# Graph network block (GGNN, then attention) on 128 small graphs: the second half of the attention's gather gets another PSUM bank, and the probability transposes and gathers move in the hand-written order

## The chip, the cores and the metric

The kernel runs on one core of one Trainium2 chip. The metric is the device time of the whole launch in microseconds, lower is better; beside it stands the profile of one execution, with its span from the first to the last instruction. The matrix engine (TensorE) is PE in the rows, VectorE is DVE, ScalarE is ACT, GpSimd is POOL, SyncE is SP.

## The reference: what is computed

128 graphs of 128 nodes with 256 features each, and an adjacency per graph. Two layers, each a residual around a ReLU of a layer norm.

```python
h = relu(layernorm(x))                       # layer 0: gated graph network, 3 steps
for i in range(3):
    m = h @ weight[i]
    aggr = einsum('bst,bsd->btd', A, m)      # sum over neighbours
    h = gru(aggr, h, w_ih, w_hh, b_ih, b_hh)
x = x + h
h = relu(layernorm(x))                       # layer 1: graph attention
Wh = h @ W.T
e = leaky_relu((Wh @ a1)[:, :, None] + (Wh @ a2)[:, None, :])
x = x + softmax(where(adj, e, -inf)) @ Wh
```

## The kernel before

**Tiles.** Four graphs make a group (128 nodes on the partitions, or 512 = 4 x 128 node columns behind 128 features). Two groups, `a` = 0 and 1, make a pair `p`; there are 16 pairs. Every product is split in fp16 high and low parts and done as three matmuls (`products`, L318 in the profile).

**Slots and steps.** A pair has six slots of eight steps. Slots 0, 2, 4 are the three GRU layers of group 0, and slots 1, 3, 5 those of group 1. The eight steps of a slot are the gate products `hn0 r0 in0 z0 hn1 r1 in1 z1`, for feature half 0 and then 1, into the PSUM banks `hn_bank`, `r_bank`, `in_bank`, `z_bank`: six matmuls of 512 columns for `hn` and `in`, twelve for `r` and `z`. This is the bulk of PE's work.

**The side work.** Everything else (layer norms, neighbour sums, transposes, the attention of the pair before) is put behind the gate step by the table `SIDE`: the key is (slot, step), an entry is (stage, arguments, offset of the pair). Every engine walks the same table and issues its own part of each stage, strictly in that order, with waits on semaphores counted by pair. `LAST_SLOT_SIDE` takes the place of slot 5 in the last pair. In pair `p` the attention of pair `p - 1` runs (offset -1), so its stages occur in 15 of the walks; the attention of the last pair is in the list `TAIL` behind all slots.

**The attention stages that the change touches.** `softmax` (ACT) writes `prob`. `probs_transpose`: PE transposes `prob` into `s_bank` (L766, four transposes), ACT copies it to `pt_hi` (L858), DVE does three short operations (L964, L965, L967) and then writes `pt_lo` from `s_bank` and `pt_hi` (L970). `gather(p, a, half)`: PE waits for `pt_lo` and multiplies two graphs of the group (twelve matmuls of 128 columns, L318) into a bank, ACT copies that to `vt_hi` (L864), DVE writes `vt_lo` (L977). Both halves use `s_bank`, so the second half's matmuls wait until DVE has written the first half's `vt_lo`. `attend` multiplies `vt` with the attention's weight into `w_bank`. `residual(p, a, c)`: PE transposes the final state into `t_bank` (L749), DVE adds it to `x_res` (L921).

**The layer norm of the next pair.** At (4, 3) `stats_gnn` makes DVE take statistics of the next pair's input, from which POOL works out the factors in eleven small operations (L295 to L312). At (4, 5) `apply_gnn` makes ACT wait for them, write `relu_gnn` (L270, four operations) and its fp16 part `h_s` (L283, two). Behind that in the table stands `neighbours(1, 2, 1)`, whose ACT part is `nb_hi` (L347) and whose DVE part is `nb_lo` (L351). At (4, 6) `split_gnn` makes DVE write the low part of `h_s` (L263, two). The DVE operation of step `in` is `n_pre` (L887).

**The state.** `update` is three DVE operations (L896, L900, L903) behind ACT's `n_out` (L824) and `tanh_z` (L828); `split_state` splits the new state for the next layer.

The order of one slot is this loop, which all engines share:

```python
for step in range(len(STEPS)):
    gate(p, slot % 2, slot // 2, STEPS[step][:-1], step // 4)
    last_slot = slot == 2 * LAYERS - 1 and not exists(p + 1)
    for stage, *which, offset in (LAST_SLOT_SIDE if last_slot else SIDE).get((slot, step), ()):
        if stage in side and exists(p + offset):
            side[stage](p + offset, *which)
```

Of the kernel before, what the change touches and what calls it, by code (L numbers as in the profile page):

```python
# [75 lines left out]
    (2, 3): [("softmax", 0, -1)],  # L76
    (2, 4): [("update", 0, 1, 0, 0), ("split_state", 0, 2, 0, 0), ("transpose", 0, 2, 0, 0)],
    (2, 5): [("neighbours", 1, 1, 1, 0)],
    (2, 6): [("probs_transpose", 0, -1)],
    (3, 0): [("update", 0, 1, 1, 0), ("split_state", 0, 2, 1, 0), ("transpose", 0, 2, 1, 0)],  # L80
    (3, 1): [("gather", 0, 0, -1)],
    (3, 2): [("neighbours", 0, 2, 0, 0), ("dots", 1, 0, -1)],
# [6 lines left out]
    (4, 2): [("neighbours", 1, 2, 0, 0), ("softmax", 1, -1)],  # L89
    (4, 3): [("stats_gnn", 0, 1)],  # L90
    (4, 4): [("update", 0, 2, 0, 0)],
    (4, 5): [("probs_transpose", 1, -1), ("apply_gnn", 0, 1), ("neighbours", 1, 2, 1, 0)],
    (4, 6): [("split_gnn", 0, 1), ("first_transpose", 0, 0, 1), ("first_transpose", 0, 1, 1)],
    (4, 7): [("gather", 1, 0, -1)],
    (5, 0): [("residual", 0, 0, 0), ("update", 0, 2, 1, 0)],
    (5, 1): [("gather", 1, 1, -1)],
    (5, 2): [("attend", 1, 0, -1), ("neighbours", 0, 0, 0, 1), ("stats_gnn", 1, 1)],
    (5, 3): [("residual", 0, 1, 0), ("attend", 1, 1, -1), ("load_att", 1, 0), ("store", 1, -1)],
    (5, 4): [("update", 1, 2, 0, 0)],
    (5, 5): [("neighbours", 0, 0, 1, 1), ("stats_att", 0, 0)],  # L100
    (5, 6): [("apply_gnn", 1, 1)],
    (5, 7): [("split_gnn", 1, 1), ("first_transpose", 1, 0, 1), ("first_transpose", 1, 1, 1), ("apply_att", 0, 0)],
}

SETUP_SIDE = {
# [9 lines left out]
        ("first_transpose", 1, 1)]  # L115

LAST_SLOT_SIDE = {
    (5, 0): [("residual", 0, 0, 0), ("update", 0, 2, 1, 0)],
    (5, 1): [("gather", 1, 1, -1), ("attend", 1, 0, -1)],
    (5, 2): [("residual", 0, 1, 0), ("stats_att", 0, 0)],  # L120
    (5, 3): [("attend", 1, 1, -1), ("load_att", 1, 0), ("store", 1, -1)],
    (5, 4): [("update", 1, 2, 0, 0), ("apply_att", 0, 0)],
# [10 lines left out]
def per_group(p, a):  # L133
    return p * 2 + a + 1


def per_chunk(p, a, c):
    return p * 4 + 2 * a + c + 1
# [6 lines left out]
def per_gate(p, a, layer, c):  # L145
    return p * 12 + 4 * layer + 2 * a + c + 1
# [10 lines left out]
def wait_reached(engine, semaphore, count):  # L157

    if not (isinstance(count, int) and count < 1):
        engine.wait_ge(semaphore, count)  # L160


def graph_blocks(nc, x, adj, weight, w_ih, w_hh, b_ih, b_hh, att_w, att_a, out):
# [5 lines left out]
    with ctx:  # L169
# [3 lines left out]
        def sem(name):  # L173
            return ctx.enter_context(nc.semaphore(name))
# [35 lines left out]
        def bank(name):  # L210
            return ctx.enter_context(nc.psum_tensor(name, [P, 512], F32))

        nb_bank, t_bank = bank("nb_bank"), bank("t_bank")
# [11 lines left out]
        nb_hi_ready, nb_lo_ready, nb_done, x1_ready = sem("nb_hi_ready"), sem("nb_lo_ready"), sem("nb_done"), sem("x1_ready")  # L225
# [88 lines left out]
        def products(bank_ap, terms, start=True, stop=True):  # L314

            todo = [m for w_hi, w_lo, d_hi, d_lo in terms for m in ((w_hi, d_hi), (w_hi, d_lo), (w_lo, d_hi))]
            for i, (w, d) in enumerate(todo):
                last = nc.tensor.matmul(bank_ap, w, d, start=start and i == 0,  # L318
                                        stop=stop and i == len(todo) - 1)
            return last  # L320
# [298 lines left out]
        hn_bank, r_bank, in_bank, z_bank = bank("hn_bank"), bank("r_bank"), bank("in_bank"), bank("z_bank")  # L619
        w_bank, s_bank = bank("w_bank"), bank("s_bank")  # L620

        def after_gates(p):

            return isinstance(p, int) and p == pairs - 1
# [2 lines left out]
            return hn_bank if after_gates(p) and a == 1 else s_bank  # L627

        def gather_bank(p, half):
            return r_bank if after_gates(p) and half == 1 else s_bank  # L630

        def attend_bank(p, half):
            return (z_bank, nb_bank)[half] if after_gates(p) else w_bank
# [19 lines left out]
        u_lo_ready, vt_lo_ready, pt_lo_ready = sem("u_lo_ready"), sem("vt_lo_ready"), sem("pt_lo_ready")  # L653
# [28 lines left out]
        with nc.Block() as block:  # L682
# [28 lines left out]
            def _(pe):  # L711
# [33 lines left out]
                def residual(p, a, c):  # L745
                    pe.wait_ge(h_ready, per_gate(p, a, LAYERS - 1, c))
                    wait_reached(pe, x1_ready, per_chunk(p, a, c) - 1)
                    for b in range(GROUP):
                        last = nc.tensor.transpose(t_bank[:, b * P:(b + 1) * P], ht[a][:, c, b * P:(b + 1) * P], ident[:])  # L749
                    last.then_inc(res_t_done, 1)  # L750
# [18 lines left out]
                def gather(p, a, half):  # L769
                    n = per_chunk(p, a, half)  # L770
                    pe.wait_ge(u_lo_ready, per_group(p, a))
                    pe.wait_ge(pt_lo_ready, per_group(p, a))
                    if after_gates(p) and half == 1:
                        pe.wait_ge(tanh_r_ready, per_gate(p, 1, LAYERS - 1, 1))
                        if a == 1:
                            pe.wait_ge(vt_lo_ready, n - 2)
                    elif half == 1:
                        pe.wait_ge(vt_lo_ready, n - 1)
                    for k in range(KC):
                        for i in range(2):  # L780
                            b = 2 * half + i
                            target = gather_bank(p, half)[:, (2 * k + i) * P:(2 * k + i + 1) * P]
                            cols = slice(k * P, (k + 1) * P)
                            last = products(target, [(u_hi[a][:, b, cols], u_lo[a][:, b, cols],
                                                      pt_hi[:, b, :], pt_lo[:, b, :])])
                    last.then_inc(gather_done, 1)

                def attend(p, a, half):
# [13 lines left out]

                all_pairs(pe, gate, {
                    "residual": residual, "neighbours": lambda *which: neighbours_pe(pe, *which), "gather": gather,
                    "scores": scores, "probs_transpose": probs_transpose, "attend": attend})

            @block.scalar
            def _(act):
# [52 lines left out]
                def gather(p, a, half):  # L861
                    act.wait_ge(gather_done, per_chunk(p, a, half))
                    wait_reached(act, attend_done, per_chunk(p, a, 0) - 1)
                    nc.scalar.activation(vt_hi[:, :, 2 * P * half:2 * P * (half + 1)],  # L864
                                         gather_bank(p, half)[:].rearrange("p (k t) -> p k t", k=KC), ACT.Copy,
                                         scale=VSCALE / (HSCALE * PSCALE)).then_inc(vt_hi_ready, 1)
# [8 lines left out]
            def _(dve):  # L875
# [98 lines left out]
                def gather(p, a, half):  # L974
                    dve.wait_ge(vt_hi_ready, per_chunk(p, a, half))
                    part = slice(2 * P * half, 2 * P * (half + 1))
                    nc.vector.scalar_tensor_tensor(vt_lo[:, :, part],  # L977
                                                   gather_bank(p, half)[:].rearrange("p (k t) -> p k t", k=KC),
                                                   VSCALE / (HSCALE * PSCALE), vt_hi[:, :, part],
                                                   ALU.mult, ALU.subtract).then_inc(vt_lo_ready, 1)  # L980
# [57 lines left out]
```

## Time and profile before

| | |
|---|---|
| device time, median of 3 runs | 1867.82 us (1867.44 to 1868.47) |
| device time of the profiled execution | 1866.37 us |
| its span | 1864.6 us |
| PE busy | 1797.0 us, 96% of the span |
| DVE busy | 1420.2 us, 76% |
| ACT busy | 1028.3 us, 55% |
| POOL busy | 346.5 us, 19% |
| mean granted clock of PE | 0.993 |

Busy time of PE is that of pipelined matmuls: the row of a 512-column matmul shows 0.38 us, but the next one starts 0.216 us later. A wait of PE is therefore best read from start to start; the idle time that the profile prints is some 0.16 us less. One pair takes about 112.7 us.

### The profile page before, as it was taken

Reading aid. Unit: us, or ns where it says so; the run is one execution under the profiler, and the core shown is the slowest. Engines: PE = TensorE matmul, PEld = TensorE weight load, DVE = VectorE, ACT = ScalarE, POOL = GpSimd, SP = SyncE. Lnnn points to the kernel's source line nnn. Section 1 sums busy time; section 2 is a strip of 40 time slices with the busy share of each in tenths; the row PEclk is TensorE's granted clock in tenths of the full one; section 3 lists DMA queues with packets and bytes.
Section 4 is the critical chain, followed back from the end, with each engine's and each line's share of the span. In section 5 each row is a group of like instructions: output and inputs, shape, how many; then the busy total and the mean of one; then the engine's idle time right before and its main releaser. Section 6 shows DMA issues by size and latency. Waiting matters only on the chain.

```text
span 1864.6 us, 32405 instructions
## 1 busy us (share of the span) xinstructions
PE 1797.0 (96%) x10620; PEld 958.6 (51%) x10620; DVE 1420.2 (76%) x2801; ACT 1028.3 (55%) x1822; POOL 346.5 (19%) x778
## 2 busy tenths in 40 slices
PE   6999999999999999999999999999999999999995
PEld 5444555545555455555545555454554545555453
DVE  6667787777877877877777877777877777877776
ACT  5555555555555546555555556555555555555543
POOL 1022030311303122030310303113031220303101
PEclk9999999999999999999999999999999999999998
DMA  3323232322313223222222313223222322323111
GB/s 103 73 63 69 52 77 48 87 59 56 87 36 90 51 52 88 56 73 51 73 68 51 93 31 101 45 56 90 56 74 45 77 70 51 73 51 84 29 47 51
DMA packets 292000, 120.50 MB, mean 65 GB/s; under 512 B 207489, under 2 KB 291969, under 8 KB 291969
## 3 DMA queue, kind: packets, MB, share of 16 engines
q1 hardware_dynamic: 291968, 120.11, 26.7%
q8 instruction: 17, 0.28, 0.1%
q14 instruction: 15, 0.11, 0.0%
HBM read 52.96 MB, written 16.78 MB: 37 GB/s over the span
## 4 chain that ended last, share of the span: by engine, by line
issue 58%; POOL 13%; DVE 9%; PE 8%; ACT 7%; DMA 3%; POOLq 1%; ACTq 0%; DVEq 0%; SPq 0%
DMA ht_s<-h_s 3%; PE z_bank L318 3%; PE r_bank L318 2%; POOL ln_gnn L310 2%; DVE n_pre L887 2%; POOL ln_att L310 2%; ACT relu_gnn L270 2%; DVE dot_terms L933 1%; PE hn_bank L318 1%; ACT tanh_r L819 1%; PE in_bank L318 1%; ACT relu_att L270 1%; DVE stats_att L248 1%; ACT u_hi L845 1%; POOL ln_att L306 1%
## 5 line engine op out<-in xcount | busy, mean ns | idle before, releaser
L824 ACT ACTIVATE n_out<-n_pre,bih 128x512 f32<-128x512 f32 x192 | 137.9, 718 | 255.0 <-DVE n_pre L887 252.8
L318 PE MATMUL hn_bank<-ht_s,wh_hi 128*128 128x512 f16 x768 | 228.4, 379 | 1.7 <-PEq L426 1.7
L318 PE MATMUL r_bank<-ht_s,wh_hi 128*128 128x512 f16 x768 | 228.4, 379 | 0.0
L318 PE MATMUL z_bank<-ht_s,wh_hi 128*128 128x512 f16 x768 | 228.4, 379 | 0.0
L882 DVE SCALAR_TENSOR_TENSOR n_pre<-tanh_r,hn_b 128x512 f32<-128x512 f32 x192 | 146.2, 761 | 68.1 <-ACT tanh_r L819 65.1
L814 ACT ACTIVATE hn_b<-hn_bank,b_hn,down 128x512 f32<-128x512 f32 x192 | 147.5, 768 | 77.8 <-PE hn_bank L318 77.8
L819 ACT ACTIVATE tanh_r<-r_bank,b_rz,down 128x512 f32<-128x512 f32 x192 | 147.4, 768 | 68.9 <-PE r_bank L318 68.8
L833 ACT ACTIVATE ht_s<-ht 128x512 f16<-128x512 f32 x128 | 80.5, 629 | 186.7 <-DVE ht L903 186.7
L351 DVE TENSOR_TENSOR nb_lo<-nb_bank,nb_hi 128x512 f16<-128x512 f32 x192 | 131.2, 683 | 67.7 <-ACT nb_hi L347 67.6
L295 POOL TENSOR_TENSOR ln_gnn<-stats_gnn 128x4 f32<-128x4 f32 x32 | 12.9, 404 | 901.9 <-DVE stats_gnn L248 901.9
L828 ACT ACTIVATE tanh_z<-z_bank,b_rz,down 128x512 f32<-128x512 f32 x192 | 146.9, 765 | 35.9 <-PE z_bank L318 35.9
L909 DVE SCALAR_TENSOR_TENSOR ht_s<-ht,ht_s 128x512 f16<-128x512 f32 x128 | 88.6, 692 | 97.1 <-ACT ht_s L833 97.1
L347 ACT ACTIVATE nb_hi<-nb_bank 128x512 f16<-128x512 f32 x192 | 113.0, 589 | 82.9 <-PE nb_bank L333 82.9
L896 DVE SCALAR_TENSOR_TENSOR diff<-ht,n_out 128x512 f32<-128x512 f32 x192 | 131.9, 687 | 30.1 <-ACT n_out L824 29.8
L900 DVE SCALAR_TENSOR_TENSOR diff<-tanh_z,diff 128x512 f32<-128x512 f32 x192 | 133.7, 696 | 15.8 <-ACT tanh_z L828 9.2
L318 PE MATMUL r_bank<-ht_s,wh_lo 128*128 128x512 f16 x384 | 145.5, 379 | 0.0
L318 PE MATMUL r_bank<-nb_hi,wi_hi 128*128 128x512 f16 x384 | 145.5, 379 | 0.0
L318 PE MATMUL r_bank<-nb_lo,wi_hi 128*128 128x512 f16 x384 | 145.5, 379 | 0.0
L318 PE MATMUL r_bank<-nb_hi,wi_lo 128*128 128x512 f16 x384 | 145.5, 379 | 0.0
L318 PE MATMUL in_bank<-nb_hi,wi_hi 128*128 128x512 f16 x384 | 145.5, 379 | 0.0
L318 PE MATMUL in_bank<-nb_lo,wi_hi 128*128 128x512 f16 x384 | 145.5, 379 | 0.0
L318 PE MATMUL in_bank<-nb_hi,wi_lo 128*128 128x512 f16 x384 | 145.5, 379 | 0.0
(180 smaller groups left out, 4053.2 us busy)
## 6 DMA issues: line engine op xcount, KB each, us to landing
x_in<-in_x_dram SPq DMA_DIRECT2D x32, 512.0 KB, 4.1
x_res<-in_x_dram SPq DMA_DIRECT2D x32, 512.0 KB, 4.1
out_dram<-x_out SPq DMA_DIRECT2D x32, 512.0 KB, 5.0
adj_in<-in_adj_dram SPq DMA_DIRECT2D x32, 256.0 KB, 4.2
adj_att<-in_adj_dram SPq DMA_DIRECT2D x32, 256.0 KB, 4.3
h_s<-ht_s SPq DMA_TRANSPOSE x128, 3.0
ht_s<-h_s SPq DMA_TRANSPOSE x64, 3.2
raw_ih<-in_L_gnn_w_ih_dram SPq DMA_DIRECT2D x2, 384.0 KB, 3.9
```

Source lines behind the costliest of these rows:

```text
L318: last = nc.tensor.matmul(bank_ap, w, d, start=start and i == 0, stop=stop and i == len(todo) - 1)
L347: nc.scalar.activation(nb_hi[a][:, c, :], nb_bank[:], ACT.Copy).then_inc(nb_hi_ready, 1)
L351: nc.vector.tensor_tensor(nb_lo[a][:, c, :], nb_bank[:], nb_hi[a][:, c, :], ALU.subtract).then_inc(nb_lo_ready, 1)
L814: nc.scalar.activation(hn_b[c][:], hn_bank[:], ACT.Identity, bias=b_hn[:, c:c + 1], scale=down_gate).then_inc(hn_ready, 1)
L819: nc.scalar.activation(tanh_r[c][:], r_bank[:], ACT.Tanh, bias=b_rz[:, c:c + 1], scale=down_half).then_inc(tanh_r_ready, 1)
L824: nc.scalar.activation(n_out[c][:], n_pre[c][:], ACT.Tanh, bias=bih[:, 4 + c:5 + c]).then_inc(n_ready, 1)
L828: nc.scalar.activation(tanh_z[c][:], z_bank[:], ACT.Tanh, bias=b_rz[:, 2 + c:3 + c], scale=down_half).then_inc(tanh_z_ready, 1)
L833: nc.scalar.activation(ht_s[layer % 2][a][:, c, 0, :], ht[a][:, c, :], ACT.Copy, scale=HSCALE).then_inc(ht_hi_ready, 1)
L882: nc.vector.scalar_tensor_tensor(n_pre[c][:], tanh_r[c][:], 1.0, hn_b[c][:], ALU.add, ALU.mult).then_inc(rn_ready, 1)
L896: nc.vector.scalar_tensor_tensor(diff[c][:], ht[a][:, c, :], 1.0 / HSCALE if layer == 0 else 1.0, n_out[c][:], ALU.mult, ALU.subtract).the ...
L900: nc.vector.scalar_tensor_tensor(diff[c][:], tanh_z[c][:], 1.0, diff[c][:], ALU.add, ALU.mult).then_inc(zdiff_ready, 1)
L909: nc.vector.scalar_tensor_tensor(ht_s[q][a][:, c, 1, :], ht[a][:, c, :], HSCALE, ht_s[q][a][:, c, 0, :], ALU.mult, ALU.subtract).then_inc( ...
```

## The change

Three edits go together. `gather_bank` gives the second half `t_bank`, the bank of the residual's transposes, in all pairs but the last (where it had `r_bank` already). The waits follow: the second half waits for what last read `t_bank` (the residual of group 1 for group 0, the second half of group 0 for group 1), and `residual` of group 0, half 0 waits for the `vt_lo` that reads `t_bank`. The table moves four things: `probs_transpose(0)` from (2, 6) to (2, 7); `probs_transpose(1)` from (4, 5), where it stood ahead of `apply_gnn`, to (4, 6), behind `split_gnn`; `gather(1, 0)` from (4, 7) and `gather(1, 1)` from (5, 1), both to (5, 0); `residual(0, 0)` from (5, 0) to (5, 1).

```diff
-    (2, 6): [("probs_transpose", 0, -1)],
-    (4, 5): [("probs_transpose", 1, -1), ("apply_gnn", 0, 1), ("neighbours", 1, 2, 1, 0)],
-    (4, 7): [("gather", 1, 0, -1)],
+    (4, 6): [("split_gnn", 0, 1), ("first_transpose", 0, 0, 1), ("first_transpose", 0, 1, 1), ("probs_transpose", 1, -1)],
+    (5, 0): [("gather", 1, 0, -1), ("gather", 1, 1, -1), ("update", 0, 2, 1, 0)],
...
         def gather_bank(p, half):
-            return r_bank if after_gates(p) and half == 1 else s_bank
+            if half == 0:
+                return s_bank
+            return r_bank if after_gates(p) else t_bank
...
                     wait_reached(pe, x1_ready, per_chunk(p, a, c) - 1)
+                    if a == 0 and c == 0:
+                        wait_reached(pe, vt_lo_ready, per_chunk(p - 1, 1, 1))
...
+                    elif half == 1 and a == 0:
+                        pe.wait_ge(x1_ready, per_chunk(p, 1, 1))
                     elif half == 1:
-                        pe.wait_ge(vt_lo_ready, n - 1)
+                        pe.wait_ge(vt_lo_ready, n - 2)
```

On ACT, from slot 4, step `r1`, to slot 5, before (line numbers are those of each kernel; the rows REGISTER_ALU and ISA are waits and counters):

```order
L819 ACTIVATE tanh_r<-r_bank,b_rz,down 128x512
L858 ACTIVATE pt_hi<-s_bank 128x512
L160 ISA
L278 ISA
L270 ACTIVATE relu_gnn<-x_in,ln_gnn 128x256 x4
L283 ACTIVATE h_s<-relu_gnn 128x512 x2
L346 REGISTER_ALU
L347 ACTIVATE nb_hi<-nb_bank 128x512
L824 ACTIVATE n_out<-n_pre,bih 128x512
L828 ACTIVATE tanh_z<-z_bank,b_rz,down 128x512
L862 REGISTER_ALU
L864 ACTIVATE vt_hi<-s_bank 128x2x256
```

and after:

```order
L824 ACTIVATE tanh_r<-r_bank,b_rz,down 128x512
L159 ISA
L277 ISA
L269 ACTIVATE relu_gnn<-x_in,ln_gnn 128x256 x4
L282 ACTIVATE h_s<-relu_gnn 128x512 x2
L345 REGISTER_ALU
L346 ACTIVATE nb_hi<-nb_bank 128x512
L863 ACTIVATE pt_hi<-s_bank 128x512
L829 ACTIVATE n_out<-n_pre,bih 128x512
L833 ACTIVATE tanh_z<-z_bank,b_rz,down 128x512
L819 ACTIVATE hn_b<-hn_bank,b_hn,down 128x512
L867 REGISTER_ALU
```

The copy `pt_hi` stood ahead of the next pair's layer norm; it now stands behind the layer norm's six operations and `nb_hi`.

On DVE, the same place, before:

```order
L882 SCALAR_TENSOR_TENSOR n_pre<-tanh_r,hn_b 128x512
L964 TENSOR_SCALAR row_live<-row_max,down 128x4
L965 RECIPROCAL row_inv<-row_sum 128x4
L967 TENSOR_TENSOR row_scale<-row_live,row_inv 128x4
L970 SCALAR_TENSOR_TENSOR pt_lo<-s_bank,pt_hi 128x512
L350 REGISTER_ALU
L351 TENSOR_TENSOR nb_lo<-nb_bank,nb_hi 128x512
L887 SCALAR_TENSOR_TENSOR n_pre<-in_bank,down,n_pre 128x512
L261 REGISTER_ALU
L263 SCALAR_TENSOR_TENSOR h_s<-relu_gnn,h_s 128x512 x2
L977 SCALAR_TENSOR_TENSOR vt_lo<-s_bank,vt_hi 128x2x256
```

and after:

```order
L887 SCALAR_TENSOR_TENSOR n_pre<-tanh_r,hn_b 128x512
L349 REGISTER_ALU
L350 TENSOR_TENSOR nb_lo<-nb_bank,nb_hi 128x512
L892 SCALAR_TENSOR_TENSOR n_pre<-in_bank,down,n_pre 128x512
L260 REGISTER_ALU
L262 SCALAR_TENSOR_TENSOR h_s<-relu_gnn,h_s 128x512 x2
L969 TENSOR_SCALAR row_live<-row_max,down 128x4
L970 RECIPROCAL row_inv<-row_sum 128x4
L972 TENSOR_TENSOR row_scale<-row_live,row_inv 128x4
L975 SCALAR_TENSOR_TENSOR pt_lo<-s_bank,pt_hi 128x512
L982 SCALAR_TENSOR_TENSOR vt_lo<-s_bank,vt_hi 128x2x256
L982 SCALAR_TENSOR_TENSOR vt_lo<-t_bank,vt_hi 128x2x256
```

`pt_lo` with its three short operations went behind `nb_lo`, `n_pre` and both `h_s`, and the two `vt_lo` now follow each other.

On ACT at the end of slot 2, before:

```order
L347 ACTIVATE nb_hi<-nb_bank 128x512
L858 ACTIVATE pt_hi<-s_bank 128x512
L824 ACTIVATE n_out<-n_pre,bih 128x512
L828 ACTIVATE tanh_z<-z_bank,b_rz,down 128x512
L814 ACTIVATE hn_b<-hn_bank,b_hn,down 128x512
```

and after:

```order
L346 ACTIVATE nb_hi<-nb_bank 128x512
L829 ACTIVATE n_out<-n_pre,bih 128x512
L833 ACTIVATE tanh_z<-z_bank,b_rz,down 128x512
L863 ACTIVATE pt_hi<-s_bank 128x512
L819 ACTIVATE hn_b<-hn_bank,b_hn,down 128x512
```

`pt_hi` went behind `n_out` and `tanh_z`. DVE's order there is unchanged: `pt_lo` stands right ahead of the three operations of `update`.

## Rows read from the trace of the kernel before

**Rows 1.** The page: busy time of each engine, share of the span, instructions

```profile
PE 1797.0 (96%) x10620; PEld 958.6 (51%) x10620; DVE 1420.2 (76%) x2801; ACT 1028.3 (55%) x1822; POOL 346.5 (19%) x778
```

**Rows 2.** Waits of PE, whole span: us in total, times, longest us

```profile
PE s_bank L318 <- DVE vt_lo L977: 22.8, 14, 1.8
PE s_bank L766 <- ACT prob L851: 12.1, 16, 5.5
PE setup_bank L484 <- DVE peaks L528: 6.6, 1, 6.6
...
PE t_bank L749 <- DVE x_res L921: 3.1, 1, 3.1
```

**Rows 3.** Timeline of PE, pair 9, slots 4 to 5: start us, us, engine, line

```profile
1131.65 0.22 PE L318 MATMUL s_bank<-pt_hi,u_hi 128*128 128x128 f16 x1
...
1132.32 0.59 PE L318 MATMUL hn_bank<-ht_s,wh_hi 128*128 128x512 f16 x2
...
1133.61 0.60 PE L749 MATMUL t_bank<-ident,ht 128*128 128x128 f32 x4
1134.05 0.59 PE L318 MATMUL r_bank<-ht_s,wh_hi 128*128 128x512 f16 x2
...
1138.37 0.22 PE L318 MATMUL s_bank<-pt_hi,u_hi 128*128 128x128 f16 x1 [1.57 <-DVE vt_lo L977]
...
1139.04 0.38 PE L318 MATMUL in_bank<-nb_hi,wi_hi 128*128 128x512 f16 x1
```

**Rows 4.** Timeline of POOL, pair 9, slot 4: the layer norm's last factor

```profile
1130.18 0.20 POOL L312 TENSOR_TENSOR ln_gnn<-ln_gnn 128x4 f32<-128x4 f32 x1
```

**Rows 5.** Timeline of ACT, same stretch

```profile
1130.41 2.08 ACT L270 ACTIVATE relu_gnn<-x_in,ln_gnn 128x256 f32<-128x256 f32 x4 [2.07 <-POOL ln_gnn L312]
...
1133.63 0.58 ACT L347 ACTIVATE nb_hi<-nb_bank 128x512 f16<-128x512 f32 x1
...
1136.92 0.58 ACT L864 ACTIVATE vt_hi<-s_bank 128x512 f16<-128x512 f32 x1
```

**Rows 6.** Timeline of DVE, same stretch

```profile
1128.60 0.22 DVE L964 TENSOR_SCALAR row_live<-row_max,down 128x4 f32<-128x4 f32 x1
...
1129.01 0.68 DVE L970 SCALAR_TENSOR_TENSOR pt_lo<-s_bank,pt_hi 128x512 f16<-128x512 f32 x1
1134.24 0.69 DVE L351 TENSOR_TENSOR nb_lo<-nb_bank,nb_hi 128x512 f16<-128x512 f32 x1 [4.55 <-ACT nb_hi L347]
...
1135.51 1.28 DVE L263 SCALAR_TENSOR_TENSOR h_s<-relu_gnn,h_s 128x512 f16<-128x512 f32 x2
1137.53 0.69 DVE L977 SCALAR_TENSOR_TENSOR vt_lo<-s_bank,vt_hi 128x512 f16<-128x512 f32 x1 [0.74 <-ACT vt_hi L864]
```

**Rows 7.** Timeline of PE, pair 2, slots 2 to 3

```profile
301.65 0.66 PE L766 MATMUL s_bank<-ident,prob 128*128 128x128 f32 x4 [0.45 <-ACT prob L851]
302.14 0.59 PE L318 MATMUL z_bank<-ht_s,wh_hi 128*128 128x512 f16 x2
...
308.61 0.22 PE L318 MATMUL s_bank<-pt_hi,u_hi 128*128 128x128 f16 x1
```

**Rows 8.** Timeline of ACT, same stretch

```profile
303.81 0.59 ACT L858 ACTIVATE pt_hi<-s_bank 128x512 f16<-128x512 f32 x1
...
306.14 0.76 ACT L828 ACTIVATE tanh_z<-z_bank,b_rz,down 128x512 f32<-128x512 f32 x1
```

**Rows 9.** Timeline of DVE, same stretch

```profile
305.81 0.68 DVE L970 SCALAR_TENSOR_TENSOR pt_lo<-s_bank,pt_hi 128x512 f16<-128x512 f32 x1
306.41 0.68 DVE L896 SCALAR_TENSOR_TENSOR diff<-ht,n_out 128x512 f32<-128x512 f32 x1
```

**Rows 10.** Stretches at a low clock: length, busy times, then PEclk

```profile
17.01:20.25 3.24, 3.24 (x10) 2.76 (x11) 3.07 (x11) 0.00 (x0) 1.67 (x10) 0.50 0.00 0
1831.95:1849.70 17.75, 5.82 (x34) 4.41 (x35) 15.02 (x52) 5.64 (x15) 4.12 (x11) 0.52 0.00 0
```

**Rows 11.** Operations of one POOL line: ns min/median/max

```profile
L306 POOL TENSOR_TENSOR ln_gnn<-ln_gnn x32: 198/200/522, 19.6 to 1711.4; 128x4 f32<-128x4 f32 x32
```

More of the change, by code:

```diff
@@ L91 @@
     (4, 4): [("update", 0, 2, 0, 0)],
-    (4, 5): [("probs_transpose", 1, -1), ("apply_gnn", 0, 1), ("neighbours", 1, 2, 1, 0)],
-    (4, 6): [("split_gnn", 0, 1), ("first_transpose", 0, 0, 1), ("first_transpose", 0, 1, 1)],
-    (4, 7): [("gather", 1, 0, -1)],
-    (5, 0): [("residual", 0, 0, 0), ("update", 0, 2, 1, 0)],
-    (5, 1): [("gather", 1, 1, -1)],
+    (4, 5): [("apply_gnn", 0, 1), ("neighbours", 1, 2, 1, 0)],
+    (4, 6): [("split_gnn", 0, 1), ("first_transpose", 0, 0, 1), ("first_transpose", 0, 1, 1), ("probs_transpose", 1, -1)],
+    (5, 0): [("gather", 1, 0, -1), ("gather", 1, 1, -1), ("update", 0, 2, 1, 0)],
+    (5, 1): [("residual", 0, 0, 0)],
     (5, 2): [("attend", 1, 0, -1), ("neighbours", 0, 0, 0, 1), ("stats_gnn", 1, 1)],
@@ L102 @@
     (5, 7): [("split_gnn", 1, 1), ("first_transpose", 1, 0, 1), ("first_transpose", 1, 1, 1), ("apply_att", 0, 0)],
+    (2, 7): [("probs_transpose", 0, -1)],
 }
@@ L117 @@
 LAST_SLOT_SIDE = {
-    (5, 0): [("residual", 0, 0, 0), ("update", 0, 2, 1, 0)],
-    (5, 1): [("gather", 1, 1, -1), ("attend", 1, 0, -1)],
+    (5, 0): [("gather", 1, 0, -1), ("gather", 1, 1, -1), ("update", 0, 2, 1, 0)],
+    (5, 1): [("residual", 0, 0, 0), ("attend", 1, 0, -1)],
     (5, 2): [("residual", 0, 1, 0), ("stats_att", 0, 0)],
```

## The prediction, made before the changed kernel ran

> **What bounds the kernel now.** I read the page's busy times first: PE is busy 96% of the span [rows 1], so the time is PE's own work plus the places where it stands still, and an edit pays or costs only what it does to those. The waits of PE come next [rows 2]. Two recur: 22.8 us in 14 waits where the second gather waits for `vt_lo`, and 12.1 us in 16 where the probability transposes wait for `prob`; one of these is the tail's 5.5 us, so the other 15 are 0.44 us each. From start to start both kinds are about 0.16 us longer: 0.60 us for the second. The setup's and the tail's waits are single ones and the change does not reach them.
>
> Then the timeline at the first wait, in a pair that stands for the others. PE issues the first gather of group 1 at 1131.65, `hn` at 1132.32, the residual's transposes at 1133.61, `r` at 1134.05. Twelve matmuls at the 0.215 us that six of `hn` show ((1133.61 - 1132.32)/6) end that at 1136.63, but the second gather starts at 1138.37: 1.74 us lost [rows 3]. The bank is the reason only in form. `vt_lo` is written at 1137.53, right behind a `vt_hi` of 1136.92 [rows 5, 6], though PE had finished that gather at 1132.3. Between them ACT was behind: it waited 2.07 us for POOL's last layer-norm factor (1130.18 to 1130.38) [rows 4], ran the layer norm, and got to `nb_hi` at 1133.63 [rows 5]; DVE sat idle 4.55 us for that `nb_hi` [rows 6]. What is late in this stretch is the chain POOL, layer norm, `nb_hi`, `nb_lo`, `n_pre`, `h_s`, and everything behind it in the order of ACT and DVE. The probability copy is not behind it now: `pt_lo` was written at 1129.01 to 1129.70 [rows 6].
>
> **The change at slots 4 to 5.** It puts the probability copy behind that chain. ACT runs `pt_hi` after `nb_hi` (ends 1134.21); 0.59 us for such a copy [rows 8], so it is there by 1134.8 and delays nobody, since ACT's next operation waits for DVE anyway. DVE is the later one: it ends the two `h_s` at 1135.51 + 1.28 = 1136.79, then the three short operations take 0.41 us (1128.60 to 1129.01) and `pt_lo` 0.68 us [rows 6]. So `pt_lo` is written at 1137.88. PE starts a gather 0.15 us after the DVE operation that releases it (1138.37 against 1138.22) [rows 3, 6], less about 0.08 us by which DVE operations overlap: 1137.95.
>
> PE meets this wait sooner. The 0.67 us of the first gather are gone from ahead of `hn`, which starts at 1131.65 and ends at 1132.94. Behind it stands the first gather now, and PE waits from 1132.94 to 1137.95: **5.0 us where it waited 1.74**. The second gather follows at once, since `t_bank` is free: that part of the change works. What PE did before its old wait, it now does after: gather 0.67, gather 0.67, `r` 2.58, transposes 0.44, and `in` starts at 1142.31 instead of 1139.04 [rows 3]. That is **3.27 us later per pair**. Nothing takes it back: what waits behind the gather on PE is all of slot 5, and a PE that is busy 96% has no slack to give. The residual's new wait is covered: both `vt_lo` follow ACT's two copies of 0.58 us and end near 1140.8, 1 us before the transposes are due at 1141.9.
>
> The old wait has 14 instances for 15 pairs, because the last pair normalises no next input; there the copy is not late and I cost the edit at nothing. 14 x 3.27 = **+45.8 us**.
>
> **The change at slots 2 to 3.** PE's 0.60 us wait for `prob` goes, as `z` covers it (twelve matmuls, 2.6 us). What is late next is `pt_lo`. ACT puts `pt_hi` behind `tanh_z`, which starts at 306.14 and is held by DVE's `n_pre`, not by PE [rows 8]. It ends at 306.90; `pt_hi` then takes until 307.40, `pt_lo` until 308.10, and the gather may start at 308.24. PE, 0.60 us earlier than before, is there at 308.61 - 0.60 = 308.01 [rows 7]. So 0.23 us comes back as a wait and 0.37 us is won. The three operations of `update` queue behind `pt_lo` on DVE and move from 306.41 to about 308.0 [rows 9]; their state is due at PE only in the neighbour product four steps on, some 8 us, and DVE's waits further on absorb the rest. 15 x 0.37 = **-5.6 us**; bounds are 0 and the whole 15 x 0.60 = 9.0.
>
> **The clock.** A 1.74 us wait has left the granted clock alone, but longer ones have not. In the setup PE waited 6.6 us for `peaks`, and the 3.24 us of work behind it ran at a granted 0.50, 1.2 GHz instead of 2.4 [rows 2, 10]. In the tail a wait of 3.1 us [rows 2] was enough: from there the clock is at 0.52 over 17.75 us, with more waits in it [rows 10]. A wait of 5.0 us lies between these two, so I expect the fall in most of the 14 pairs. The setup row prices one at half of 3.24 us, 1.6 us; the fall can come late or be back early in some pairs, so I take 1.4. 14 x 1.4 = **+19.6 us**; bounds are 0 (no fall) and twice that, if the slow stretch is twice as long as in the setup.
>
> The Trainium skill, "TensorE: Matmul & The Clock Gate", section "HAM oscillation — how this bites in real kernels", says that a long enough wait that recurs in each tile puts the engine back to its slow clock in each of them, where otherwise the price is paid once. By that rule the term stands as worked out; by the clock before, 0.993 over the span, it would be zero. It speaks against this change, and the trace shows the fall but only outside the loop.
>
> **Sum.** 1866.4 (the profiled execution) + 45.8 - 5.6 + 19.6 = 1926.2. The median is 1.4 us above that execution, so **1928 us**, 3.2% slower.
>
> **The rivals.**
>
> *The clock stays up.* The loop's waits have not moved it so far, and PE is dense on both sides of this one. Against it: the tail's 3.1 us. Time: 1928 - 19.6 = 1908. Chance 0.20.
>
> *Worse than the sum.* The slow clock lasts twice as long: 1928 + 19.6 = 1948. For it: rows 10 show stretches longer than one. Against it: PE is full behind the wait here. Chance 0.09.
>
> *Faster: the second bank does what it says.* If `pt_lo` were there when `hn` ends, both recurring waits would go: 14 x 1.74 + 9.0 = 33.4, or 1834 us. The point from which this decides: `in` must start no later than 1139.04, so the gather by 1139.04 - 0.44 - 2.58 - 1.34 = 1134.68, 3.27 us before my 1137.95. That needs the POOL chain to be over that much sooner. For it: DVE's short operations leave its neighbourhood, and one POOL operation takes 0.20 or 0.52 us [rows 11]; that gives 0.3 us, not 3.3, or 14 x 0.32 = 4.5 us in all. Chance 0.05.
>
> The Trainium skill, "PSUM — Partial Sum Buffer", section "Summary: rules for kernel authors", advises another bank where one engine reads and the matmul runs. By it alone the old wait is a bank's wait and the time is the 1834 above; the rows say that the bank was free late because ACT and DVE were late.
>
> *No change.* The same mechanism at its break-even, with the chain 3 us earlier: 1868. Chance 0.03.
>
> **Chances and range.** My forecast, wait and clock, has 0.63. Faster by over 0.2% (3.7 us, about what this kernel's runs can tell from no change) 0.05, within 0.03, slower 0.92, all the rest. The range must leave out no more than 2 in 10: it takes in the clock's lower case less the 4.5 us of POOL, 1908 - 4.5 = 1904, and goes up to 1944, short of the doubled clock. **1904 to 1944.**
>
> **What would show it.** In the changed profile: the wait of PE before the first gather on `s_bank`, for `pt_lo`, 14 times at about 4.9 us, some 68 us in total; no wait for `vt_lo` in the loop; none for `prob` but the tail's; 15 short ones of 0.1 to 0.3 us for `pt_lo` in slot 3. Mean granted clock near 0.983 (14 stretches of 2.8 us at half speed, 39 us, off the 0.993 of before); 0.993 would make the rival with the full clock right. On DVE `pt_lo` ends some 7.6 us after POOL's last factor starts. I am wrong if PE's waits at the gathers total less than 30 us, or if `nb_hi` no longer waits for the layer norm. A wait of the residual's transposes for `vt_lo` would mean that I cut its 1 us of cover too fine.

## The result, and the profile after

The changed kernel takes 1939.17 us (median of 4 runs, 1938.56 to 1940.94) against 1867.78 us: a ratio of 1.0383, 95% interval 1.0365 to 1.0401. It is 3.8% slower; the prediction was 1928 us, between 1904 and 1944.

The page of the changed kernel, the lines that answer to [rows 1]:

```profile
span 1937.2 us, 32419 instructions
...
PE 1827.3 (94%) x10620; PEld 979.5 (51%) x10620; DVE 1421.4 (73%) x2801; ACT 1025.9 (53%) x1822; POOL 343.8 (18%) x778
```

PE runs the same 10620 matmuls and is busy 30.3 us longer for them (1797.0 before). That is work at a lower clock; the rest of the 72.6 us of span is standing still. The waits of PE, over the whole span, answer to [rows 2]:

```profile
PE s_bank L317 <- DVE pt_lo L975: 70.4, 23, 5.2
PE setup_bank L483 <- DVE peaks L527: 6.5, 1, 6.5
PE s_bank L769 <- ACT prob L856: 5.5, 1, 5.5
```

Both waits of before are gone from the loop: none for `vt_lo`, and for `prob` only the tail's. In their place PE waits for `pt_lo`, 14 long waits and the short ones that the profile counts. From start to start the long ones are 5.01 us in 11 pairs and 5.29 to 5.40 in 3, 71.1 us together, where the waits for `vt_lo` were 25.1. The timeline of PE, pair 9, slots 4 to 5, as [rows 3]:

```profile
1174.57 0.38 PE L317 MATMUL hn_bank<-ht_s,wh_lo 128*128 128x512 f16 x1
1180.08 0.26 PE L317 MATMUL s_bank<-pt_hi,u_hi 128*128 128x128 f16 x1 [5.13 <-DVE pt_lo L975]
...
1181.32 0.31 PE L317 MATMUL t_bank<-pt_hi,u_hi 128*128 128x128 f16 x1
...
1182.60 0.87 PE L317 MATMUL r_bank<-ht_s,wh_hi 128*128 128x512 f16 x2
...
1185.46 0.60 PE L752 MATMUL t_bank<-ident,ht 128*128 128x128 f32 x4
1185.90 0.38 PE L317 MATMUL in_bank<-nb_hi,wi_hi 128*128 128x512 f16 x1
```

The second gather follows the first without a wait, and the residual's transposes do not wait either: the new bank does what it is for. But the first gather takes 1.24 us instead of 0.67, and `r` 2.86 instead of 2.58, because the clock is down. ACT and DVE in the same stretch, as [rows 5, 6]:

```profile
1172.54 2.07 ACT L269 ACTIVATE relu_gnn<-x_in,ln_gnn 128x256 f32<-128x256 f32 x4 [2.83 <-POOL ln_gnn L311]
...
1175.76 0.58 ACT L346 ACTIVATE nb_hi<-nb_bank 128x512 f16<-128x512 f32 x1
1176.24 0.59 ACT L863 ACTIVATE pt_hi<-s_bank 128x512 f16<-128x512 f32 x1
```

```profile
1176.37 0.69 DVE L350 TENSOR_TENSOR nb_lo<-nb_bank,nb_hi 128x512 f16<-128x512 f32 x1 [5.84 <-ACT nb_hi L346]
...
1177.64 1.28 DVE L262 SCALAR_TENSOR_TENSOR h_s<-relu_gnn,h_s 128x512 f16<-128x512 f32 x2
1178.84 0.22 DVE L969 TENSOR_SCALAR row_live<-row_max,down 128x4 f32<-128x4 f32 x1
...
1179.26 0.68 DVE L975 SCALAR_TENSOR_TENSOR pt_lo<-s_bank,pt_hi 128x512 f16<-128x512 f32 x1
...
1183.47 0.69 DVE L982 SCALAR_TENSOR_TENSOR vt_lo<-t_bank,vt_hi 128x512 f16<-128x512 f32 x1 [0.59 <-ACT vt_hi L869]
```

`pt_lo` ends at 1179.94, 0.14 us before PE starts and 7.6 us after POOL's last factor starts (1172.31). It stands behind the layer norm, `nb_hi`, `nb_lo`, `n_pre` and both `h_s`. The granted clock (the number behind the five engines' busy times, 1.00 for 2.4 GHz and 0.50 for 1.2) in this pair, in the one before it, and between:

```profile
1179.70:1183.20 3.50, 3.12 (x26) 2.84 (x27) 0.93 (x2) 1.07 (x3) 0.00 (x0) 0.51 0.78 150
1060.30:1067.10 6.80, 5.62 (x32) 3.72 (x33) 3.86 (x10) 2.10 (x4) 0.00 (x0) 0.50 0.40 77
1067.10:1179.70 112.60, 107.60 (x626) 56.37 (x624) 84.23 (x168) 61.58 (x110) 21.98 (x48) 1.00 0.24 61
```

The clock falls to 1.2 GHz once in each of the 14 pairs, for 3.4 us in seven and 6.8 us in the other seven. Its mean is 0.976; the prediction had 0.983. In the loop the distance between neighbouring matmuls shows the same 14 falls (0.43 us for 512 columns where 0.216 is usual). In the setup of this trace, and of the one of experiment 3, matmuls also stand 0.43 us apart though the clock's record says 1.00, so these two means leave a slow stretch of the setup out.

### The profile page after: what moved, and what is told of

Its sections match the earlier page's. It is cut to its first block, busy times and chain, and to the rows that moved or that the text cites. A ratio compares the mean times of both kernels' runs of the same rounds, so it can differ in the third digit from the quotient of the medians.

```text
span 1937.2 us, 32419 instructions
## 1 busy us (share of the span) xinstructions
PE 1827.3 (94%) x10620; PEld 979.5 (51%) x10620; DVE 1421.4 (73%) x2801; ACT 1025.9 (53%) x1822; POOL 343.8 (18%) x778
## 4 chain that ended last, share of the span: by engine, by line
issue 59%; POOL 12%; DVE 8%; PE 8%; ACT 6%; DMA 2%; POOLq 1%; ACTq 0%; DVEq 0%; SPq 0%
DMA ht_s<-h_s 2%; PE z_bank L317 2%; PE r_bank L317 2%; POOL ln_gnn L309 2%; DVE n_pre L892 2%; POOL ln_att L309 2%; ACT relu_gnn L269 2%; DVE dot_terms L938 1%; PE hn_bank L317 1%; PE in_bank L317 1%; ACT tanh_r L824 1%; ACT relu_att L269 1%; DVE stats_att L247 1%; ACT u_hi L850 1%; POOL ln_att L305 1%
## 5 line engine op out<-in xcount | busy, mean ns | idle before, releaser
L317 PE MATMUL r_bank<-ht_s,wh_hi 128*128 128x512 f16 x768 | 237.8, 392 | 0.0
L887 DVE SCALAR_TENSOR_TENSOR n_pre<-tanh_r,hn_b 128x512 f32<-128x512 f32 x192 | 142.3, 741 | 90.2 <-ACT tanh_r L824 86.9
L317 PE MATMUL r_bank<-ht_s,wh_lo 128*128 128x512 f16 x384 | 149.4, 389 | 0.0
```

The costliest lines, as they stand in the source:

```text
L887: nc.vector.scalar_tensor_tensor(n_pre[c][:], tanh_r[c][:], 1.0, hn_b[c][:], ALU.add, ALU.mult).then_inc(rn_ready, 1)
```

## The experiments

The theory: `pt_lo`, put behind the layer norm of the next pair on ACT and DVE, is late, and PE's longer wait also costs clock. The rivals: the moved gathers and the bank's new waits cost the time; the clock costs little; and, of the kernel before, that the shared bank was what its wait was for.

**1. The probability transposes of group 1 put back ahead of the layer norm, in the changed kernel.**

```diff
-    (4, 5): [("apply_gnn", 0, 1), ("neighbours", 1, 2, 1, 0)],
+    (4, 5): [("probs_transpose", 1, -1), ("apply_gnn", 0, 1), ("neighbours", 1, 2, 1, 0)],
-    (4, 6): [("split_gnn", 0, 1), ("first_transpose", 0, 0, 1), ("first_transpose", 0, 1, 1), ("probs_transpose", 1, -1)],
+    (4, 6): [("split_gnn", 0, 1), ("first_transpose", 0, 0, 1), ("first_transpose", 0, 1, 1)],
```

> The changed kernel, but the probability transposes of group 1 stand at (4, 5) ahead of the layer norm again, as before the change; gathers, banks and group 0 as changed. My theory (pt_lo behind the layer norm is what costs): the 5.0 us wait at the first gather goes from all 14 pairs. What is late in its place is vt_lo of the second half, for which the residual's transposes now wait: ACT reaches the two vt_hi only behind tanh_z and hn_b, the second vt_lo ends some 2.8 us after PE comes to the transposes. Time about 1867.8 + 14 x 1.05 - 4.5 = 1878 with the clock up; up to 1909 if a wait of 2.8 us lets it fall. Rival (the moved gathers and the wait on the transposes' bank are what costs): stays above 1925.

Measured: 1889.99 us, ratio 1.0099 (1.0075 to 1.0123). PE's waits:

```profile
PE t_bank L752 <- DVE vt_lo L982: 38.2, 14, 2.9
```

The long wait for `pt_lo` is gone and with it 49 us (1939.17 to 1889.99), so the place of `pt_lo` is the cause of the larger part. The wait that takes its place stands where it was expected, 2.77 to 3.06 us from start to start, 40.4 us in all where the changed kernel had 71.1. The time lies 12 us over the sum at a full clock: the clock fell after 7 of the 14 waits, for 3.4 us each, and half of that is 11.9 us. What is left is 22 us over the kernel before. By the traces it is 15.3 us of longer waits and the 11.9 of clock, less 4.4 that the move of group 0 gains (experiment 2): the price of the moved gathers and their new bank.

**2. The probability transposes of group 0 one step later, alone, in the kernel before.**

```diff
-    (2, 6): [("probs_transpose", 0, -1)],
+    (2, 7): [("probs_transpose", 0, -1)],
```

> The kernel before with only the probability transposes of group 0 moved one step later. My theory: 15 waits of 0.60 us become 15 waits of pt_lo of about 0.31 us in the next slot, as the changed kernel's trace shows: 15 x 0.29 = 4.4 us faster, about 1863.4. Rival (the work that this delays on DVE costs as much again): 1867 to 1869.

Measured: 1862.73 us over 8 runs, ratio 0.9966 (0.9953 to 0.9979). In the trace 15 waits of 0.60 us for `prob` (9.0 us) are replaced by 15 of 0.31 us for `pt_lo` (4.6 us). This part of the change is a gain. By the trace it is half of the wait that it removes (4.4 us); the time says 6.4 us, with an interval from 3.9 to 8.8.

**3. Filler matmuls in the wait of the changed kernel.** The 20 extra matmuls are overwritten by the second gather; the output is not changed.

```diff
+FILL = 20
...
+                    if a == 1 and half == 0 and not after_gates(p):
+                        pe.wait_ge(vt_lo_ready, n - 1)
+                        for i in range(FILL):
+                            nc.tensor.matmul(t_bank[:], wh_hi[:, 0, 0:P], nb_hi[1][:, 0, :], start=True, stop=True)
                     pe.wait_ge(pt_lo_ready, per_group(p, a))
```

> The changed kernel with 20 extra matmuls of 512 columns (4.3 us, their result is overwritten) on PE ahead of its wait for pt_lo at the first gather of group 1. They fit in the 5.0 us wait, so they add no time of their own; the output is as before. My theory: the clock stays at full in the loop, the wait shrinks to 0.7 us, and what the changed kernel loses to the clock comes back: 72.6 us in all less 41.3 us for the waits is 31 us, so about 1908. Rival (the clock costs little and the rest is waiting elsewhere): 1930 or more. If the extra matmuls delay the work behind them, over 1939.

Measured: 1912.77 us, ratio 1.0229 (1.0206 to 1.0252). PE's wait and, for the pair in the middle of the span, the granted clock:

```profile
PE s_bank L318 <- DVE pt_lo L980: 7.3, 14, 0.7
```

```profile
1150.00:1175.00 25.00, 24.56 (x162) 14.19 (x161) 17.04 (x32) 11.74 (x19) 7.65 (x19) 1.00 0.11 21
```

With 4.3 us of useless work put into each wait the kernel is 26 us faster by the two times, and 29 us (1.5%) by the two ratios, which are 0.0154 apart: the clock did not fall in the loop at all (mean 0.994). The trace of the changed kernel gives a third figure: PE was at work in 61.8 us of its 14 slow stretches, and half of that is 31 us. So the clock is worth 26 to 31 us of the changed kernel's time. What is left, 42.8 us by the ratio, agrees with the waits: 46.0 us more at the gathers less the 4.4 of experiment 2 is 41.6.

**4. In the kernel before, the neighbour sums ahead of `apply_gnn`.** One entry of the table changes place; banks and gathers stay.

```diff
-    (4, 5): [("probs_transpose", 1, -1), ("apply_gnn", 0, 1), ("neighbours", 1, 2, 1, 0)],
+    (4, 5): [("probs_transpose", 1, -1), ("neighbours", 1, 2, 1, 0), ("apply_gnn", 0, 1)],
```

> The kernel before with one entry moved: at (4, 5) the neighbour sums stand ahead of apply_gnn. My theory (ACT's layer norm, waiting for POOL, holds nb_hi and all behind it): nb_hi, nb_lo and n_pre come 5 us sooner, vt_lo ends by 1136.3 in the pair of the rows, before PE arrives at 1136.6, and the 14 waits of 1.74 us vanish: about 1843. Rival (the bank shared by the two gathers is the limit): the waits stay, 1866 to 1869.

Measured: 1843.41 us, ratio 0.9853 (0.9831 to 0.9875). The wait for `vt_lo` is gone from the loop. ACT and DVE in pair 9:

```profile
1114.85 0.60 ACT L347 ACTIVATE nb_hi<-nb_bank 128x512 f16<-128x512 f32 x1
1117.32 2.07 ACT L270 ACTIVATE relu_gnn<-x_in,ln_gnn 128x256 f32<-128x256 f32 x4 [1.87 <-POOL ln_gnn L312]
```

```profile
1116.83 0.74 DVE L887 SCALAR_TENSOR_TENSOR n_pre<-in_bank,down,n_pre 128x512 f32<-128x512 f32 x1
...
1122.43 0.69 DVE L977 SCALAR_TENSOR_TENSOR vt_lo<-s_bank,vt_hi 128x512 f16<-128x512 f32 x1 [0.47 <-ACT vt_hi L864]
```

The second gather of group 1 on PE:

```profile
1123.26 0.22 PE L318 MATMUL s_bank<-pt_hi,u_hi 128*128 128x128 f16 x1
```

`nb_hi` now runs while POOL still works on the factors, and `vt_lo` starts 5.1 us after the layer norm's start on ACT (1117.32) instead of 7.1 (1130.41 and 1137.53 in [rows 5, 6]). It ends at 1123.12, 0.14 us before the second gather starts, so the wait is gone with almost nothing to spare. Both gathers still share one bank: one bank is enough when its reader is on time. The reverse is not shown. All eight banks of the kernel have a use, and a second bank that nothing else holds, which would let the second gather start whatever the reader does, was not tried in the kernel before.

**5. The bank alone, in the kernel before.** The table is untouched; the waits are what this order needs. The residual's transposes also wait for the `vt_lo` that reads `t_bank` (left out below).

```diff
-            return r_bank if after_gates(p) and half == 1 else s_bank
+            if half == 0:
+                return s_bank
+            return r_bank if after_gates(p) else t_bank
...
                     elif half == 1:
-                        pe.wait_ge(vt_lo_ready, n - 1)
+                        pe.wait_ge(x1_ready, per_chunk(p + 1, 0, 0))
```

> The kernel before, its table untouched; only the second half of the gather goes to the bank of the residual's transposes, with the waits that this order needs (the gather of group 1 waits for the residual of group 0, half 0; the later transposes wait for the gather's vt_lo). My theory: the bank alone takes no wait away. The gather is now released by DVE's residual, which stands right behind vt_lo in DVE's order and ends 0.6 us after it (1138.82 against 1138.22 in the pair of the rows): 14 x 0.6 = 8 us slower, about 1876. Rival (the shared bank was the limit): the 14 waits go, about 1843.

Measured: 1883.76 us, ratio 1.0091 (1.0076 to 1.0107).

```profile
PE t_bank L318 <- DVE x_res L929: 30.9, 14, 2.4
```

The waits are 2.24 to 2.58 us from start to start, 33.1 us together against 25.1: the 8 us that were expected. The other 8 us were not: the clock fell after 5 of the 14, for 3.4 us each, and half of that is 8.5 us. So moving the wait to this bank costs time in the old order, because in this order the bank is held until the residual's `x_res` behind `vt_lo` is done. Two of the stretches behind the waits, the first after one of 2.24 us, the second after the one of 2.58:

```profile
1035.70:1039.10 3.40, 3.40 (x13) 1.74 (x12) 3.37 (x5) 0.42 (x1) 1.41 (x1) 0.50 0.32 61
922.00:925.40 3.40, 3.40 (x33) 2.44 (x31) 3.36 (x4) 0.64 (x2) 1.40 (x1) 1.00 0.42 82
```

**6. The changed kernel with the neighbour sums ahead of `apply_gnn`**, `pt_lo` still behind `h_s`.

```diff
-    (4, 5): [("apply_gnn", 0, 1), ("neighbours", 1, 2, 1, 0)],
+    (4, 5): [("neighbours", 1, 2, 1, 0), ("apply_gnn", 0, 1)],
```

> The changed kernel with the neighbour sums ahead of apply_gnn at (4, 5). Of the chain ahead of pt_lo only nb_hi, nb_lo and n_pre are gone; the layer norm and h_s stay. My theory: pt_lo comes 1.8 us sooner, the wait at the first gather shrinks from 5.0 to about 3.3 us: 1867.8 + 14 x 1.53 - 4.4 = 1885 at the full clock. Waits of 2.8 to 3.05 us let the clock fall in 7 of 14 cases in the run with the transposes put back, those of 5 us in 14 of 14; I expect some 10 falls at 1.8 us: 1903, and between 1885 and 1911. Rival (the length of the wait does not matter to the clock): 14 falls, 1911 or more, or none, 1885.

Measured: 1900.58 us, ratio 1.018 (1.0164 to 1.0195). The waits are 3.27 us in 8 pairs and 3.56 in 6, and the clock fell after 10, for 3.4 us each: the 10 falls that were expected, and a time 2 us under the expected one.

**7. The changed kernel with both ahead of `apply_gnn`.**

```diff
-    (4, 5): [("apply_gnn", 0, 1), ("neighbours", 1, 2, 1, 0)],
+    (4, 5): [("probs_transpose", 1, -1), ("neighbours", 1, 2, 1, 0), ("apply_gnn", 0, 1)],
-    (4, 6): [("split_gnn", 0, 1), ("first_transpose", 0, 0, 1), ("first_transpose", 0, 1, 1), ("probs_transpose", 1, -1)],
+    (4, 6): [("split_gnn", 0, 1), ("first_transpose", 0, 0, 1), ("first_transpose", 0, 1, 1)],
```

> The changed kernel with both the probability transposes of group 1 and the neighbour sums ahead of apply_gnn at (4, 5). My theory: no wait at either gather; the residual's transposes wait some 0.8 us for the second vt_lo, since hn_b stands ahead of both vt_hi on ACT: 1867.8 - 24.6 - 4.4 + 11 = 1850, clock up. Rival (the moved gathers and the bank cost nothing once the chain is early): 1839.

Measured: 1849.86 us, ratio 0.9907 (0.9892 to 0.9922).

```profile
PE t_bank L752 <- DVE vt_lo L982: 8.8, 14, 0.9
```

With the chain early, the changed banks and gathers are faster than the kernel before. But they are 12 us slower than the next run, and the one wait that they add, on the residual's transposes, is 11.1 us of that from start to start.

**8. The two small moves together, on the kernel before**, the edits of 2 and 4.

> The kernel before with two entries moved and no bank changed: the neighbour sums ahead of apply_gnn at (4, 5), and the probability transposes of group 0 one step later. My theory: the two gains add, 1867.8 - 24.4 - 5 = 1838. Rival (with PE ahead by more, the waits in slots 2 and 3 come back larger): 1843.

Measured: 1837.75 us over 5 runs, ratio 0.9843 (0.983 to 0.9857), the fastest here. In its loop PE waits for neither `prob` nor `vt_lo`; what is left is 15 waits of 0.31 us for `pt_lo` and 15 of 0.26 for `nb_lo`, both from start to start. PE is now busy 98% of the span:

```profile
PE 1796.0 (98%) x10620; PEld 960.8 (52%) x10620; DVE 1411.3 (77%) x2801; ACT 1020.2 (56%) x1822; POOL 349.8 (19%) x778
```

## Why the prediction was right

**What bounds the kernel.** Right, and experiment 4 shows it: the 22.8 us of waits [rows 2] named the bank's reader, but the lateness came from ACT, which stood in the layer norm with the neighbour sums behind it. That "the bank is the reason only in form" says more than was shown: the wait needed both, a late reader and a shared bank.

**Slots 4 to 5.** The step was predicted from rows of the kernel before and came out to a tenth: a wait of 5.01 us in most pairs where 5.0 was said, `pt_lo` ready 7.6 us after POOL's last factor, as said, and 46.0 us more waiting in all (71.1 less 25.1) for a term of 45.8. The pair shown above is one of the three longer ones, at 5.29. POOL's operation L306 did become faster in it (0.20 us instead of 0.52), but the chain did not: its first operation, L295, took 0.91 us instead of 0.31. The second `vt_lo` ended at 1184.16 and the transposes came at 1185.46, so the cover of 1 us held, at 1.3 with the clock down. At the full clock of experiment 3 it was 1.1 (`vt_lo` ends at 1163.84, the transposes start at 1164.92).

**Slots 2 to 3.** The wait for `prob` vanished from all 15 pairs and returned as 0.31 us for `pt_lo`, not 0.23. The term was -5.6 us; the traces give 9.0 - 4.6 = 4.4, and experiment 2 measured 0.34%, 6.4 us, with an interval from 0.21% to 0.47% that holds both.

**The clock.** The mechanism was right and its size too small. The clock fell after all 14 waits, for a term of 19.6 us that should have been 26 to 31: 1.9 to 2.2 us per fall, not 1.4. Two things went into that. I had taken less than the setup's row gave, on the guess that some falls would be shortened. And I took the 3.24 us of work [rows 10] for the length of the slow stretch, which it is not:

```profile
13.43:20.26 6.83, 3.25 (x10) 2.77 (x11) 6.65 (x14) 0.00 (x0) 1.68 (x10) 0.50 0.21 57
```

In the setup of the kernel before, the clock was down for 6.8 us, from 3.6 us before PE started again. A stretch costs half of the part in which PE works. In the changed kernel that part was 3.1 to 3.4 us in the seven short stretches, but 5.2 to 5.8 in the seven long ones. The clock's term was 6 to 11 us too small, and slots 2 to 3 add 1.2 us. That is the 11 us by which the result lies over the forecast; it is 5 us inside the range. The full-clock rival, 1908, is what experiment 3 built: 1912.77. The rival with the slow stretch twice as long, 1948, had a chance of 0.09; its time misses by 9 us, but the stretch was twice as long in half of the pairs, for a reason that I had not given.

**The rivals.** The faster one fails where it was said to decide: against the point from which the change gains, the first gather started 3.3 us too late in most pairs. The Trainium skill's page "TensorE: Matmul & The Clock Gate" (section "HAM oscillation — how this bites in real kernels") says that a long wait in every tile costs the clock in every tile, and this trace agrees inside the loop: 14 falls in 14 pairs. The Trainium skill's page "PSUM — Partial Sum Buffer" (section "Summary: rules for kernel authors") asks for a different bank when PSUM is read while matmuls run. It promises no time. Taken as a price, as the prediction's rival did, it is not borne out by the bank used here: alone it cost 0.9% (experiment 5), while experiment 4 gained 1.5% without another bank.

## What to carry to other kernels

When an engine waits for the reader of a buffer, look at why the reader is late before giving the writer another buffer: here one neighbour in ACT's order, moved ahead of a wait for GpSimd, removed the wait, while the second bank at hand, which has a reader of its own further down the order, made it longer. When a second bank is proposed, look at who holds it and until when. Before a short operation is moved down a hand-written order, list on each engine what it is moved behind and when that is released; here the rows of the old trace gave the new wait to a tenth of a microsecond in 11 of 14 pairs. And price a recurring wait of the matrix engine above its length, since the clock may be lost on top.

## What the runs showed of the hardware

I had not expected that the clock answers to the length of a recurring wait by degrees. With dense work on both sides, the granted clock fell to 1.2 GHz after 0 of 14 waits of 1.73 to 2.01 us (before), 5 of 14 of 2.24 to 2.58 us (experiment 5), 7 of 14 of 2.77 to 3.06 us (experiment 1), 10 of 14 of 3.27 to 3.56 us (experiment 6), and 14 of 14 of 5.0 to 5.4 us (the changed kernel).

The length alone does not decide. Waits of one length in one kernel differ in it, and in experiment 5 the clock fell after 4 of 8 waits of 2.24 us but after only 1 of 6 of 2.52 to 2.58.

In the first three groups with falls the slow stretch was 3.4 us each time; after 5 us it was 6.8 us in every second pair. The short and the long ones of the changed kernel begin at different places: the short ones from 0.4 us before to 0.4 us after PE starts again, the long ones 1.1 to 1.7 us before. Why they take turns was not tried. One fall cost 1.7 us (half of 3.4) behind waits of up to 3.6 us, where PE was at work all through the stretch; behind the waits of 5 us it cost 1.5 to 1.7 us in the short stretches and 2.6 to 2.9 in the long ones.
